# Expert phase of an attention and mixture-of-experts kernel: four tiles deep instead of two, and one more wait before each scatter

## What is computed

```python
tokens = layernorm(x).reshape(-1, 256)
topk_idx, topk_w = _route(tokens, router_weight, router_bias)      # 4 of 32 experts
gate_vals = silu(einsum('th,eih->tei', tokens, gate_w))            # e: expert, i: 128
up_vals = einsum('th,eih->tei', tokens, up_w)
expert_out = einsum('tei,ehi->teh', gate_vals * up_vals, down_w)
mixed = (take(expert_out, topk_idx) * topk_w[:, :, None]).sum(1)
shared = (silu(h @ shared_gate_w.T) * (h @ shared_up_w.T)) @ shared_down_w.T
out = x + mixed + shared
```

## Time and profile before

| | us |
|---|---|
| median of 3 runs | 1436.4 |
| lowest, highest | 1429.46, 1436.93 |
| the profiled execution, its own time | 1446.11 |
| its span, first to last instruction | 1444.1 |

### The profile page before, as it was taken

How to read it: one execution, slowest core, us unless ns; L and a number is a source line. 1 busy time by engine, 2 the same in 40 slices (tenths; PEclk the granted TensorE clock), 3 DMA queues, 4 the chain that set the end, 5 groups by cost and what they waited for, 6 DMA issues and landing times.

```text
span 1444.1 us, 33057 instructions
## 1 busy us (share of the span) xinstructions
PE 1341.7 (93%) x8730; PEld 1042.9 (72%) x8730; DVE 963.0 (67%) x4500; ACT 1042.4 (72%) x2861; POOL 610.4 (42%) x662
## 2 busy tenths in 40 slices
PE   7999999999999999999798989988888889989997
PEld 4666666666666676666587878878788878878886
DVE  5578888888888888887863444444444444447888
ACT  5999999999999999998515555555555655553432
POOL 1004544544444554454553555555555555550000
PEclk8999999999999999999899999999999999999998
DMA  7145455445445544544865444444444444419886
GB/s 263 71 144 179 144 182 189 148 146 181 163 137 177 181 139 155 181 150 163 317 206 188 142 144 146 145 143 138 146 143 144 145 137 142 119 31 339 302 296 228
DMA packets 145780, 246.78 MB, mean 171 GB/s; under 512 B 22075, under 2 KB 108477, under 8 KB 144960
## 3 DMA queue, kind: packets, MB, share of 16 engines
q1 hardware_dynamic: 119488, 177.25, 37.9%
q0 software_dynamic: 26112, 67.42, 13.5%
HBM read 104.30 MB, written 120.09 MB: 155 GB/s over the span
## 4 chain that ended last, share of the span: by engine, by line
PE 51%; ACT 35%; issue 9%; DVE 3%; another core or an unknown queue 1%; DMA 0%; POOL 0%; ACTq 0%; SPq 0%; DVEq 0%; POOLq 0%
PE psT L1018 10%; PE psS L1028 9%; PE ps L1018 9%; ACT arena L1151 7%; PE ps L901 5%; ACT arena L1159 5%; PE ps L1009 5%; PE psS L912 4%; ACT arena L1167 3%; ACT arena L1119 3%; ACT arena L1123 2%; ACT arena L1074 2%; PE psT L901 2%; ACT arena L1111 2%; ACT arena L1103 2%
## 5 line engine op out<-in xcount | busy, mean ns | idle before, releaser
L686 POOL DMA_INDIRECT expert_out<-pay,dest x288 | 283.7, 985 | 259.6 <-DVE pay L1866 100.0
L546 POOL DMA_INDIRECT lists<-pay,slot x168 | 171.4, 1021 | 212.1 <-PE psT L812 39.4
L1028 PE MATMUL psS<-arena,history 128*128 x576 | 182.1, 398 | 52.0 <-DVE history L1859 31.0
L1866 DVE TENSOR_SCALAR pay<-psS,dest 128x256 f32<-128x256 f32 x288 | 138.5, 481 | 85.6 <-PE psS L1028 80.1
L1018 PEld LDWEIGHTS ps<-pad,hist_j 128*128 128x128 f32 x1152 | 150.2, 194 | 17.8 <-ACT pad L1310 6.7
L1018 PEld LDWEIGHTS psT<-pad 128*128 128x128 f32 x1152 | 150.3, 193 | 14.8 <-ACT pad L1310 5.1
L1018 PE MATMUL ps<-pad,hist_j 128*128 128x128 f32 x1152 | 155.5, 278 | 3.6 <-ACT pad L1310 3.3
L1018 PE MATMUL psT<-pad 128*128 128x128 f32 x1152 | 154.4, 277 | 2.9 <-ACT pad L1310 2.7
L1028 PEld LDWEIGHTS psS<-arena,history 128*128 128x128 f32 x576 | 87.2, 191 | 70.2 <-issue 69.2
L546 POOL DMA_INDIRECT lists<-arena,slot x88 | 90.0, 1023 | 95.9 <-PE psT L812 21.2
L742 PE MATMUL ps<-arena 128*128 128x512 f32 x256 | 127.3, 620 | 2.0 <-ACT arena L1111 1.8
(11 more groups left out here) (238 smaller groups left out, 3320.6 us busy)
## 6 DMA issues: line engine op xcount, KB each, us to landing
lists<-pad SPq DMA_DIRECT2D x72, 516.0 KB, 6.2
pay<-lists SPq DMA_DIRECT2D x288, 129.0 KB
arena<-expert_out SPq DMA_DIRECT2D x32, 1024.0 KB, 6.8
pay<-pay SPq DMA_DIRECT2D x42, 384.0 KB
x<-in_x SPq DMA_DIRECT2D x32, 256.0 KB
out<-arena SPq DMA_DIRECT2D x32, 256.0 KB, 5.7
arena<-arena SPq DMA_DIRECT2D x20, 384.0 KB
arena<-in_ctx SPq DMA_DIRECT2D x32, 192.0 KB
```

Of the source, the lines that this page charges most:

```text
L546: pool.indirect_dma_start(lists, bass.IndirectOffsetOnAxis(ap=slots(u)[:, j, k:k + 1], axis=0), paid(u)[:, j, k, :], None).then_inc(scat[3 ...
L686: pool.indirect_dma_start(expert_out, bass.IndirectOffsetOnAxis(ap=dest[:, t % DESTS, 1:2], axis=0), yy[n], None, bounds_check=T * TOPK - ...
L1028: pe.matmul(dbank[n % 2][:, 0:D], hh[:, n % 4, :], w_dn[:, at(e, 1), :].rearrange("p a n -> p (a n)"), start=True, stop=True)\
L1866: dve.tensor_scalar(yy[n], dbank[n % 2][:, 0:D], dest[:, t % DESTS, 0:1].bitcast(fp32), None, ALU.mult)\
```

## The change

Turned rows, weight copies and gate-and-up banks get four places each, the third and fourth in memory that the expert stage doesn't use otherwise (the mask rows, and a new tensor that holds the attention bias and the mask bytes). The two banks of `turn_x` and the two of `down_proj` stay two. PE, ACT and DVE run four tiles ahead (`AHEAD`) with turns and copies, and three behind (`BEHIND`) with the down product and its weighing. SILU writes straight into `hh`, and DVE multiplies it in place. ACT's table reads go eight tiles ahead. `scatter_tile(t)` waits also for `gu_full` to reach t + 3.

```diff
--- before.py
+++ after.py
@@ -78,6 +78,8 @@
 B_LINKS, A_LINKS, S_LINKS = 4, 7, 10
 BLANK_UNIT = 16 * 2 * TOPK // FILL
 WARM = 20
+AHEAD = 4
+BEHIND = 3
 MADE = 16
 DESTS = 16
 EARLY = 8
@@ -156,14 +158,16 @@
         w_dn = arena[:, E * 2 * D:E * 3 * D].rearrange("p (e n) -> p e n", e=E)
 
         pay = sb("pay", [P, 4, TOPK, ROW])
-        mask_u8 = sb("mask_u8", [DH + 1, 4, 2, P], u8)
-        mask_row = sb("mask_row", [DH + 1, 2, 2, 2 * P], bf16)
+        mask_row_all = sb("mask_row", [P, 2, 2, 2 * P], bf16)
+        mask_row = mask_row_all[0:DH + 1]
+        bo_mask = sb("bo_mask", [P, 2 * D])
+        bo_b = bo_mask[:, 0:D]
+        mask_u8 = bo_mask[0:DH + 1, D:2 * D].bitcast(u8).rearrange("p (a j n) -> p a j n", a=4, j=2)
         ones_sq = sb("ones_sq", [P, P], bf16)
         tri = sb("tri", [P, P], bf16)
         gain = sb("gain", [P, 13])
         gl, bl, gx, bx = gain[:, 0:2], gain[:, 2:4], gain[:, 4:7], gain[:, 7:10]
         gq, gk, gqk = gain[:, 10:11], gain[:, 11:12], gain[:, 12:13]
-        bo_b = sb("bo_b", [P, D])
         rb_b = sb("rb_b", [P, 1, E])
         stats = sb("stats", [P, 6, 6])
 
@@ -265,14 +269,15 @@
         xs = [rows[:, n, :] for n in range(SLOTS)]
         yy = [rows[:, SLOTS + n, 0:D] for n in range(SLOTS)]
         flat_p = pad.rearrange("p k n -> p (k n)")
-        xsT = flat_p[:, 0:2 * D].rearrange("p (b n) -> p b n", b=2)
-
-
-        w_now = [flat_p[:, 2 * D:4 * D].rearrange("p (k n) -> p k n", k=2),
-                 hist_j[:, :].bitcast(fp32).rearrange("p (k n) -> p k n", k=2)]
         flat_h = history.rearrange("p u e -> p (u e)")
-        sg = flat_h[:, 0:4 * I].rearrange("p (b n) -> p b n", b=4)
-        hh = flat_h[:, 4 * I:8 * I].rearrange("p (b n) -> p b n", b=4)
+        hh = flat_h[:, 0:4 * I].rearrange("p (b n) -> p b n", b=4)
+        xsT = [flat_p[:, 0:D], flat_p[:, D:2 * D], flat_h[:, 4 * I:6 * I], flat_h[:, 6 * I:8 * I]]
+
+
+        w_now = [v.rearrange("p (k n) -> p k n", k=2)
+                 for v in (hist_j[:, :].bitcast(fp32), flat_p[:, 2 * D:4 * D],
+                           mask_row_all.rearrange("p a j n -> p (a j n)").bitcast(fp32), bo_mask[:, :])]
+        gu_bank = [ps[2], ps[3], ps[4], psO]
         xs_in = [sem(f"xs_in{n}") for n in range(SLOTS)]
         dest_kept, w_ready = sem("dest_kept"), sem("w_ready")
         xst_full, xst_ev, gu_full = sem("xst_full"), sem("xst_ev"), sem("gu_full")
@@ -683,6 +688,7 @@
             def scatter_tile(t, n):
                 pool.wait_ge(dest_kept, t + 1)
                 pool.wait_ge(yy_done, t + 1)
+                pool.wait_ge(gu_full, upto(t + 3, TILES))
                 pool.indirect_dma_start(
                     expert_out, bass.IndirectOffsetOnAxis(ap=dest[:, t % DESTS, 1:2], axis=0),
                     yy[n], None, bounds_check=T * TOPK - 1, oob_is_err=False).then_inc(y_out[n], 16)
@@ -1012,12 +1018,12 @@
             def gate_up(t, n):
                 pe.wait_ge(xst_ev, t + 1)
                 pe.wait_ge(w_ready, t + 1)
-                ge(pe, hh_done, t - 1)
+                ge(pe, hh_done, t - 3)
                 for which in range(2):
                     for k in range(2):
-                        m = pe.matmul(ps[2 + n % 2][:, which * P:(which + 1) * P],
-                                      w_now[1 - n % 2][:, k, which * I:(which + 1) * I],
-                                      xsT[:, n % 2, k * P:(k + 1) * P], start=k == 0, stop=k == 1)
+                        m = pe.matmul(gu_bank[n % 4][:, which * P:(which + 1) * P],
+                                      w_now[n % 4][:, k, which * I:(which + 1) * I],
+                                      xsT[n % 4][:, k * P:(k + 1) * P], start=k == 0, stop=k == 1)
                 m.then_inc(gu_full, 1)
 
             def down_proj(t, n, e):
@@ -1029,25 +1035,25 @@
                           w_dn[:, at(e, 1), :].rearrange("p a n -> p (a n)"), start=True, stop=True)\
                   .then_inc(dn_full, 1)
 
-            expert_regs = [pe.alloc_register(f"expert{d}") for d in range(4)]
+            expert_regs = [pe.alloc_register(f"expert{d}") for d in range(AHEAD)]
             expert = {}
 
             def read_expert(t):
 
-                reg = expert_regs[t % 4]
+                reg = expert_regs[t % AHEAD]
                 pe.load(reg, tab[0:1, t:t + 1])
                 expert[t] = pe.snap(reg, min_val=0, max_val=E - 1)
 
-            turn_x(0, 0)
-            turn_x(1, 1)
-            for t in range(TILES + 1):
+            for t in range(AHEAD):
+                turn_x(t, t)
+            for t in range(TILES + BEHIND):
                 if t < TILES:
                     gate_up(t, t % SLOTS)
                     read_expert(t)
-                if t + 2 < TILES:
-                    turn_x(t + 2, (t + 2) % SLOTS)
-                if t >= 1:
-                    down_proj(t - 1, (t - 1) % SLOTS, expert[t - 1])
+                if t + AHEAD < TILES:
+                    turn_x(t + AHEAD, (t + AHEAD) % SLOTS)
+                if t >= BEHIND:
+                    down_proj(t - BEHIND, (t - BEHIND) % SLOTS, expert[t - BEHIND])
 
 
             pe.wait_ge(yy_done, TILES)
@@ -1306,41 +1312,42 @@
                 act.wait_ge(xst_full, t + 1)
                 if t == 0:
                     act.wait_ge(sd_full, 2 * EARLY)
-                ge(act, gu_full, t - 1)
-                act.activation(xsT[:, n % 2, :], ps[n % 2][:, 0:D], ACT.Copy).then_inc(xst_ev, 1)
+                ge(act, gu_full, t - 3)
+                act.activation(xsT[n % 4], ps[n % 2][:, 0:D], ACT.Copy).then_inc(xst_ev, 1)
 
             def weights_copy(t, n, e):
 
-                ge(act, gu_full, t - 1)
-                act.activation(w_now[1 - n % 2], w_gu[:, at(e, 1)].rearrange("p a k n -> p (a k) n"), ACT.Copy)\
+                ge(act, gu_full, t - 3)
+                act.activation(w_now[n % 4], w_gu[:, at(e, 1)].rearrange("p a k n -> p (a k) n"), ACT.Copy)\
                    .then_inc(w_ready, 1)
 
             def gate_silu(t, n):
                 act.wait_ge(gu_full, t + 1)
-                ge(act, hh_done, t - 3)
-                act.activation(sg[:, n % 4, :], ps[2 + n % 2][:, 0:P], ACT.Silu).then_inc(sg_done, 1)
-
-            expert_regs = [act.alloc_register(f"next_expert{d}") for d in range(4)]
+                ge(act, dn_full, t - 3)
+                act.activation(hh[:, n % 4, :], gu_bank[n % 4][:, 0:P], ACT.Silu).then_inc(sg_done, 1)
+
+            expert_regs = [act.alloc_register(f"next_expert{d}") for d in range(2 * AHEAD)]
             expert = {}
 
             def read_expert(t):
 
-                reg = expert_regs[t % 4]
+                reg = expert_regs[t % (2 * AHEAD)]
                 act.load(reg, tab[0:1, t:t + 1])
                 expert[t] = act.snap(reg, min_val=0, max_val=E - 1)
 
-            for t in range(4):
+            for t in range(AHEAD):
                 read_expert(t)
-            for t in range(2):
+            for t in range(AHEAD):
                 weights_copy(t, t, expert[t])
                 rows_copy(t, t)
+                read_expert(t + AHEAD)
             for t in range(TILES):
                 gate_silu(t, t % SLOTS)
-                if t + 2 < TILES:
-                    weights_copy(t + 2, (t + 2) % SLOTS, expert[t + 2])
-                    rows_copy(t + 2, (t + 2) % SLOTS)
-                if t + 4 < TILES:
-                    read_expert(t + 4)
+                if t + AHEAD < TILES:
+                    weights_copy(t + AHEAD, (t + AHEAD) % SLOTS, expert[t + AHEAD])
+                    rows_copy(t + AHEAD, (t + AHEAD) % SLOTS)
+                if t + 2 * AHEAD < TILES:
+                    read_expert(t + 2 * AHEAD)
 
 
             act.wait_ge(dn_full, TILES)
@@ -1855,8 +1862,7 @@
 
             def hidden(t, n):
                 dve.wait_ge(sg_done, t + 1)
-                ge(dve, dn_full, t - 3)
-                dve.tensor_tensor(hh[:, n % 4, :], sg[:, n % 4, :], ps[2 + n % 2][:, P:2 * P], ALU.mult)\
+                dve.tensor_tensor(hh[:, n % 4, :], hh[:, n % 4, :], gu_bank[n % 4][:, P:2 * P], ALU.mult)\
                    .then_inc(hh_done, 1)
 
             def weigh_result(t, n):
@@ -1871,15 +1877,15 @@
                 ge(dve, y_out[n], left(t - (DESTS - SLOTS)))
                 dve.tensor_copy(dest[:, t % DESTS, :], xs[n][:, D:ROW].bitcast(i32)).then_inc(dest_kept, 1)
 
-            for t in range(4):
+            for t in range(AHEAD):
                 keep_dest(t, t)
-            for t in range(TILES + 1):
+            for t in range(TILES + BEHIND):
                 if t < TILES:
                     hidden(t, t % SLOTS)
-                if t + 4 < TILES:
-                    keep_dest(t + 4, (t + 4) % SLOTS)
-                if t >= 1:
-                    weigh_result(t - 1, (t - 1) % SLOTS)
+                if t + AHEAD < TILES:
+                    keep_dest(t + AHEAD, (t + AHEAD) % SLOTS)
+                if t >= BEHIND:
+                    weigh_result(t - BEHIND, (t - BEHIND) % SLOTS)
 
 
```

## The result

| | before | changed |
|---|---|---|
| median, us | 1434.54 | 1456.54 |
| lowest, highest (4 runs each) | 1429.46, 1436.93 | 1451.41, 1461.13 |
| the profiled execution, its own time | 1446.11 | 1461.13 |
| its span | 1444.1 | 1459.1 |

What follows compares the result with a forecast made beforehand. PE was taken as the bound, with 86.9 us of expert-stage waiting on its late signals. Terms -59.3, +2.8, +1 and 0 sum to -55.5 us, so 1436.4 becomes 1380.9 us; own range 1365 to 1400, overall 1350 to 1450.

Steps and rivals of the forecast that it cites:

- The bound and its reading: Expert stage: PE's own rate is 1.543 us a tile; 86.9 us is PE waiting, put down to its late signals.
- Term 1: Expert stage: reserve grows from 1.0 to 1.9 us, each gap loses up to 0.92 if holds stay; -59.3 us.
- longer runs, longer holds: Rival, expert stage: PE no longer pauses, every scatter run is at least three, holds grow; +15.6 + 3.8, 1456 us; chance 0.20.
- Term 2: Start of expert stage: four turns, not two, precede the first product, which waits for the fourth tile's rows; +2.8 us.
- Term 3: End of expert stage: four down products follow the last gate_up without waiting, last scatter 1 to 2 us later; +1 us.
- Term 4: POOL's scatter in the expert stage: its new wait for t + 3 is always met already and paces nothing; 0 us.
- the first rival: Expert stage: evenly spaced results keep holds short, so all 86.9 us of PE waiting goes; 1353 us; chance 0.20.
- the rhythm of runs is the bound: Rival, expert stage: scatter runs and holes set the rate and PE only trails; stage unchanged, 1440 us; chance 0.14.
- slower: Rival, expert stage: longer scatter runs bring longer holds; +15.6 us in the stage, 1456 us in all; chance 0.20.
- All waiting goes: Rival, expert stage: 1.9 us of reserve covers the short holds, all 86.9 us of waiting vanishes; 1353 us; chance 0.20.
- The other rule: Repeated gaps on the busy engine in the expert stage mean too few buffers; all of the idle time goes with buffers.

Runs made afterwards that it cites:

- part 4 of b_mix2: Kernel before on a late chip, last 72 tiles with plain stores by SP instead of POOL's scatters: 1.561 us a tile; whole run 1411.59 against 1457.16.
- a_again: The changed kernel, unaltered, on a quick chip: 1362.55 against the kernel before's 1361.11 us, ratio 1.0008.
- a_mix5's part 2: Changed kernel on a late chip, 72 tiles with the scatter's wait at t + 5 instead of t + 3: 1.741 us a tile; whole run 1428.69 against 1438.51.
- a_both: Changed kernel with the scatter's wait at t + 5 and two turns before the first product, late chip: 1423.82 against the kernel before's 1439.25 us, ratio 0.9897.
- b_pace3: Kernel before with the scatter's wait for t + 3 added, quick chip: ratio 1.0012 to the kernel before; repeated on a second quick chip, 1.002.
- a_start2: Changed kernel with two turns instead of four ahead of the first product, quick chip: 1361.8 against the kernel before's 1360.6 us, ratio 1.001.

## Why the prediction was wrong

**The bound and its reading** were right as far as they went: PE's own rate of 1.543 is what a quick chip gives throughout, the 86.9 us are late signals, and part 4 of b_mix2 shows that they go with POOL's scatters. The cause was "inferred from this coincidence", and a_again shows what the inference lacked: the coincidence of two things, runs and a late chip.

**Term 1 failed, and with it the forecast.** Its two halves have to be told apart. Where the idle time would stand was right: before the turn (73.9 us in the page, 62.5 of them ended by `rows_copy`), the pair that stayed a pair. What failed is "if the holds stay as they are". They grew with the reserve: 61 over 1.9 us instead of 25. The mechanism is the rival's, "longer runs, longer holds": PE runs on during a hold, so when the signal comes ACT has four products to work off, 0.94 to 1.19 us apart (1063.12, 1064.07, 1065.01, 1066.20), faster than POOL's 1.29. That makes a run of four scatters, and the next hold ends only after the run (of the 61, 48 start in the hole behind a run whose last scatter has ended). A cycle before: 2 x 1.29 + 3.08 = 5.66 us for three tiles, 1.89 a tile. Changed: 3 x 1.29 + 3.70 = 7.57 for four, 1.89. The extra depth went into a longer cycle of the same rate. So -59.3 became +2.7 in the traces; even if the 7.0 us that no trace places were all the stage's, it would be +9.7. That the run's length is what counts is shown from the other side: a_mix5's part 2 and a_both cut it back to three at the new depth, 2 x 1.29 + 2.57 = 5.15, 1.72 a tile. The kernel before had runs of three too, but with the longer hole of 3.08; what shortens it isn't shown.

**Term 2** was right in place, short in size: 4.6 instead of 2.8. I took over the fourth tile's rows at 764.83 from the trace before. They stand behind SP's last weight load there too, but from the issue of that load to the third tile's rows it took 6.8 us in that trace and 8.9 in the changed kernel's, which is the difference. That time varies from trace to trace whatever the kernel (two deep 7.5 in b_pace3 and 8.5 in b_pace3_again, four deep 8.7 in a_again and 7.0 in a_start2). The upper bound that I gave (+2.8) should have left room for it.

**Term 3** was short: 5.9 instead of 1 (bounds 0 and 2). The last scatter does come later against the last product (8.1 instead of 4.4 us). Two of its steps failed. The down products behind the last `gate_up` were said to "need no wait: 0 for PE", but they wait for their pair of banks, and the last of them starts 2.3 us later against that `gate_up`. And PE's signals to the next stage are held while the backlog of scatters runs, 1.5 and 1.4 us at two steps; I had priced the late signals in the stage and put them at nothing behind it.

**Term 4** held: the wait for t + 3 is met at least 3.13 us before each scatter of the changed kernel's trace starts, by the modelled ends of the products. A late signal doesn't change that: the weighed rows come from a down product that PE issues later, and in the stretch above PE's held signals arrive in PE's order. Taking the wait away gave 0.9993, on a quick chip. Its remark that a wait that did pace POOL would give the first rival's time was wrong: the true wait of a_both leaves 53.5 us of waiting, where the changed kernel had 89.5 on its chip.

**The rivals.** The stage followed *the rhythm of runs is the bound* (+3.8 forecast over all, its stage at nothing; measured +2.7); the whole time, 1456.54, is what *slower* gave (1456), but that is luck: by the traces the stage is smaller and start and end are larger (+2.7 against +15.6, +10.5 against +3.8), and 7.0 us of the difference of the medians has no place. Its mechanism is seen, its price wasn't. *All waiting goes* is ruled out on late chips; on quick ones there is nothing to go.

**The other rule** named in the prediction, that repeated gaps on the busy engine can mean too few buffers (the Trainium skill, Perfetto Trace Analysis, Optimization Strategy): this case disagrees, on the late chip of the pair, with twice the buffers and 89.5 us of gaps instead of 86.9.

**What stays open.** Why PE's signals are late on some chips, and what in POOL's scatters holds them: their number, POOL's time in them or their DMA queue. One count goes with the kind of chip: outside the parts without scatters, the traces of the late chips hold 1110 to 1160 recorded semaphore updates per 100 us in the first stage and 800 to 1230 in the expert stage, those of the quick ones 1500 to 1610 and, without extra stores, 2480 to 2710. That is a correlation only. It leaves a rival untested: that the recording itself plays a part in the late signals, since every execution here has recorded spans and none is on record without.

## What to carry to other kernels

When a stall is a cycle between two engines (a burst on one delays a signal, the delay makes the next burst), a deeper buffer can lengthen the burst and leave the rate, as it did here; price depth on the cycle, (run + hole) / tiles, before taking the reserve off each gap. What went with a gain here was a bound on the burst: a wait for a product that is still under way, not for one that order already guarantees. Look at the kernel before on several chips before explaining a stall of its trace, and price what a longer prologue and epilogue meet, not only the steady stage.

## What the runs showed of the hardware

- There were two kinds of chips, 5 to 7% apart on the same kernel (1360.4 to 1365.6 and 1434.5 to 1457.2 us). On the late ones, while POOL issues indirect DMAs nearly back to back, PE's signals reach ACT up to 4.16 us late with ACT free (the trace of the kernel before), and then several together, 0.18 us apart. With plain stores by SP in their place one SILU in 72 was late.
- A scatter of 64 rows takes POOL 0.908 us, one of 128 rows 0.985.
- Two extra stores a tile of 128 rows of 4 bytes (576 in all) cost 204 us: DMA share 1.08 at 122 GB/s. They also made a few of PE's signals late on a quick chip (5 of 288, up to 1.84 us).
